# A two-layer attention and top-2 expert kernel: expert sums fetched token by token through device memory, and V projected last in layer 0

## The chip, the cores and the metric

The kernel runs on one core of one Trainium2 chip. The metric is the device time of the whole program in microseconds (us): lower is better. A measurement of this kernel can tell some 2% from no change.

## The reference

256 tokens (a 16x16 grid) of 192 numbers go through two layers. Each layer is attention with 12 heads of 16, then a mixture of 8 experts, of which each token uses its best two:

```python
x = x + conv0(ln(x))        # qkv, scores + relative position terms (rows, columns), softmax, projection
t = ln(x); x = x + t + sum_e w_e * down_e(silu(gate_e t) * up_e t)      # layer 0: hidden 432 ... 1584
x = x + conv1(ln(x))        # the same attention without relative terms
t = ln(x); x = x + t + sum_e w_e * (w2_e relu(w1_e t + b1_e) + b2_e)    # layer 1: hidden 768 each
```

Here w_e is the router's softmax value of a chosen expert (in layer 1 divided by the sum of the two), and 0 for the six others. All data are float32.

## The kernel before, in words

Everything is written by hand for five engines, each with its own instruction list, and the only ties are semaphores. TensorE (PE) does all products. An f32 matmul shows as two records in the trace, a transpose as one.

**Attention.** `attend` projects K, Q and V with `project` and `project_tokens`. In layer 0, 32 small products (L1036) then form the relative position terms from Q, one for each row and each column of the grid, 48 columns each, in banks 5, 6, 7 and 3. ScalarE (ACT) copies the row terms (L503), VectorE (DVE) adds the column terms (L655) and rounds (L657), GpSimd (POOL) makes the remainder (L424), and only then may `scores` (L970) start. `keep_clock` (L916) puts products of ones into places where PE would idle. Then, two heads at a time: scores, row maximum on DVE (L661), exponential on ACT (L517), transposes (L985), copies, and `weigh` (L997), the product with V.

**Experts.** The router's two choices per token give each token a place in its expert's list of at most 96 `SLOTS`. `gather` (L1122) collects the tokens of each expert by products with one-hot matrices. Then the experts run in steps of 128 hidden units (layer 0: 60 steps; layer 1: 8 x 3 steps of 256), written as (e, t). A step on PE is `first_products` (L1135, L1137, L1139) and, `LAG` steps later, `down` (L1150). ACT and DVE make the hidden values in between (L475, L750 in layer 0; L481, L753 in layer 1). When an expert's sum is complete, DVE copies it out of PSUM (L739, `copy_y`), and PE brings it back to the tokens in `combine` (L1158): two products with `weightedT`, the one-hot matrix times the router's weight, into bank 4, where the sum over experts is kept. POOL makes those matrices for all 8 experts (L435), PE transposes them two experts at a time (L1167, `turn_weighted`), and DVE and ACT copy them (L732, L464).

An expert with over 96 tokens gets a further job in layer 1; in these data there is one (three more steps at the end). Which jobs there are is found on DVE beside the first steps: `list_jobs`, `number_jobs` (L787 to L795), `place_jobs`. SyncE (SP) issues all DMAs in the order of its list; in layer 1 it reads the job list and loads the job's weights.

## Time and profile before

| | us |
|---|---|
| median of 3 runs | 238.82 (236.95 to 240.77) |
| the profiled execution | 235.63 |
| its span, first to last instruction | 233.6 |
| PE busy | 216.7 (93%) |
| DVE busy | 103.6 (44%) |
| ACT busy | 68.5 (29%) |
| POOL busy | 37.0 (16%) |
| mean granted TensorE clock | 0.957 of full speed |

The profile is of one execution; its time includes 2.0 us outside the span. Busy time of matmuls is modelled and overlaps, so differences between the starts of instructions say more than their durations.

### The profile page before, as it was taken

The page shows a single profiled execution, that of the slowest core. Times are in us where ns is not written, and L with a number is a line of the kernel's source. Part 1 is how long each engine was busy: PE and PEld are TensorE (multiplying, and loading weights), DVE is VectorE, ACT ScalarE, POOL GpSimd, SP SyncE. Part 2 cuts the span into 40 slices and gives each one's busy share as a digit, 9 for nine tenths or more (in the row PEclk, how much of TensorE's full clock was granted, in tenths as well). Part 3 has the DMA queues.
Part 4 walks back from the last instruction along what each step waited for, and adds up shares of the span by engine and source line. Part 5 has one row for each costly group of instructions (what it writes and reads, how often), then busy time and mean ns, then how long its engine had stood idle before and what let it go on. Part 6 is the DMA issues. An engine that isn't in the chain of part 4 may idle for free.

```text
span 233.6 us, 4218 instructions
## 1 busy us (share of the span) xinstructions
PE 216.7 (93%) x1580; PEld 195.1 (84%) x1580; DVE 103.6 (44%) x334; ACT 68.5 (29%) x197; POOL 37.0 (16%) x60
## 2 busy tenths in 40 slices
PE   7999989869999999999999989799869999999992
PEld 7799877549898999999999789575558999999991
DVE  2340687568623122222222234886569564723221
ACT  2031087525221212222222131666522021211100
POOL 5220300011990000000000014000014950000000
PEclk9996799997999999999999999958999999999997
DMA  6999999936000000000000000999900000500001
GB/s 169 349 425 423 438 454 424 440 140 153 0 3 0 3 0 0 3 1 0 3 0 0 3 6 15 369 425 426 385 6 1 0 0 15 191 0 3 0 3 41
DMA packets 4492, 31.05 MB, mean 133 GB/s; under 512 B 584, under 2 KB 2064, under 8 KB 2192
## 3 DMA queue, kind: packets, MB, share of 16 engines
q1 hardware_dynamic: 4464, 30.69, 33.6%
q8 instruction: 15, 0.25, 0.5%
q14 instruction: 13, 0.11, 0.1%
HBM read 30.50 MB, written 0.20 MB: 131 GB/s over the span
## 4 chain that ended last, share of the span: by engine, by line
PE 90%; ACT 4%; issue 2%; DVE 2%; POOL 0%; DVEq 0%; ACTq 0%; POOLq 0%
PE bank L1150 17%; PE bank L1137 13%; PE bank L916 9%; PE bank L1135 8%; PE bank L1139 7%; PE bank L985 6%; PE bank L1158 5%; PE bank L940 5%; PE bank L1036 4%; PE bank L970 4%; PE bank L997 3%; PE bank L1122 3%; PE bank L1167 1%; ACT scratch L517 1%; DVE neg_max L661 1%
## 5 line engine op out<-in xcount | busy, mean ns | idle before, releaser
L1150 PE MATMUL bank<-w,scratch 128*96 128x192 f32 (+2 forms) x228 | 52.0, 330 | 0.1
L1137 PE MATMUL bank<-xe_lo,w 128*128 128x192 f32 (+3 forms) x168 | 43.3, 339 | 0.0
L750 DVE TENSOR_TENSOR scratch<-scratch,bank 128x96 f32<-128x96 f32 (+5 forms) x60 | 15.2, 253 | 52.8 <-ACT scratch L475 52.8
L1150 PEld LDWEIGHTS bank<-w,scratch 128*96 128x96 f32 (+2 forms) x228 | 30.7, 164 | 1.5 <-issue 0.3
L475 ACT ACTIVATE scratch<-bank 128x96 f32<-128x96 f32 (+5 forms) x60 | 15.0, 249 | 55.3 <-PE bank L1139 55.3
L1135 PE MATMUL bank<-scratch,w 128*128 128x96 f32 (+3 forms) x168 | 30.8, 265 | 0.0
L1135 PEld LDWEIGHTS bank<-scratch,w 128*128 128x128 f32 (+3 forms) x168 | 27.7, 185 | 3.0 <-issue 3.0
L1139 PE MATMUL bank<-scratch,w 128*128 128x96 f32 (+3 forms) x168 | 29.9, 259 | 0.0
L1139 PEld LDWEIGHTS bank<-scratch,w 128*128 128x128 f32 (+3 forms) x168 | 29.0, 185 | 0.4
L517 ACT ACTIVATE scratch<-bank,neg_max 128x256 f32<-128x256 f32 x48 | 19.8, 477 | 18.9 <-DVE neg_max L661 18.9
L1137 PEld LDWEIGHTS bank<-xe_lo,w 128*128 128x128 f32 (+3 forms) x168 | 24.9, 187 | 0.0
L435 POOL TENSOR_SCALAR scratch<-const,place,gate 128x96 f32<-128x96 f32 x32 | 22.0, 702 | 5.2 <-issue 5.1
L916 PE MATMUL bank<-ones 128*128 128x128 f32 x134 | 21.4, 327 | 1.4 <-POOL ones L393 1.4
L404 POOL TENSOR_TENSOR rstd<-var_eps,const 128x2 f32<-128x2 f32 x4 | 2.8, 706 | 119.8 <-DVE var_eps L593 119.8
L916 PEld LDWEIGHTS bank<-ones 128*128 128x128 f32 x134 | 20.3, 239 | 1.4 <-POOL ones L393 1.4
L985 PE MATMUL bank<-const,scratch 128*128 128x128 f32 x96 | 16.4, 307 | 3.8 <-ACT scratch L517 1.7
L661 DVE TENSOR_REDUCE neg_max<-bank 128x2 f32<-128x512 f32 x24 | 15.7, 683 | 6.5 <-PE bank L970 6.5
L985 PEld LDWEIGHTS bank<-const,scratch 128*128 128x128 f32 x96 | 11.3, 152 | 8.3 <-ACT scratch L517 4.2
L481 ACT ACTIVATE scratch<-bank,bias 128x96 f32<-128x96 f32 x24 | 6.9, 336 | 32.2 <-PE bank L1139 32.2
L753 DVE TENSOR_SCALAR scratch<-bank,bias 128x96 f32<-128x96 f32 x24 | 6.5, 313 | 17.6 <-PE bank L1139 17.5
L1158 PE MATMUL bank<-scratch 96*128 96x192 f32 x64 | 13.1, 327 | 0.4 <-DVE scratch L739 0.4
L671 DVE COPY scratch<-bank 128x512 f32<-128x512 f32 x16 | 10.9, 684 | 3.5 <-PE bank L985 3.5
(160 smaller groups left out, 254.4 us busy)
## 6 DMA issues: line engine op xcount, KB each, us to landing
w<-experts_dram SPq DMA_DIRECT2D x9, 1152.0 KB, 12.3
w<-experts_dram SPq DMA_DIRECT2D x1, 3624.0 KB, 41.8
w<-experts_dram SPq DMA_DIRECT2D x1, 3024.0 KB, 33.7
w<-experts_dram SPq DMA_DIRECT2D x1, 2496.0 KB, 26.6
w<-experts_dram SPq DMA_DIRECT2D x1, 2016.0 KB, 21.2
w<-experts_dram SPq DMA_DIRECT2D x1, 1704.0 KB, 16.9
w<-experts_dram SPq DMA_DIRECT2D x1, 1416.0 KB, 12.2
w<-experts_dram SPq DMA_DIRECT2D x1, 1272.0 KB, 9.3
```

What stands on the lines that cost most here:

```text
L435: nc.gpsimd.tensor_scalar(weighted[:, t, e, :], places, place[:, t, e:e + 1], gate[:, t, e:e + 1], ALU.is_equal, ALU.mult).then_inc(weight ...
L475: nc.scalar.activation(silu_g[0:m, n % 2, :], up_bank(n)[0:m, 0], ACT.Silu).then_inc(sems["silu_ready"], 1)
L517: nc.scalar.activation(probs[:, h % HB, t, :], bank[h % HB][:, t * TOK:(t + 1) * TOK], ACT.Exp, bias=neg_max[:, h, t:t + 1]).then_inc(prob ...
L661: nc.vector.tensor_reduce(neg_max[:, h, :], bank[h % HB][:].rearrange("p (t k) -> p t k", t=TT), AX_X, ALU.max, negate=True).then_inc(max_ ...
L750: nc.vector.tensor_tensor(hidden[0:m, n % RING, 0], silu_g[0:m, n % 2, :], up_bank(n)[0:m, 1], ALU.mult).then_inc(sems["hidden_vec"], 1)
L916: nc.tensor.matmul(bank[b][:, 0:P], ones[:], ones[:], start=True, stop=True)
L985: last = nc.tensor.transpose(bank[4 + head % 2][:, at:at + P], probs[:, h % HB, t, k * P:(k + 1) * P], ident)
L1135: nc.tensor.matmul(tile[:, 0], w0[:, begin + long[0]:begin + long[0] + m], hi, start=True, stop=False, skip_group_check=True)
L1137: nc.tensor.matmul(tile.rearrange("p u s -> p (u s)"), w0[:, begin + short:begin + short + m], lo.rearrange("p u s -> p (u s)"), start=Fal ...
L1139: return nc.tensor.matmul(tile[:, 1], w0[:, begin + long[1]:begin + long[1] + m], hi, start=False, stop=True, skip_group_check=True)
L1150: ins = nc.tensor.matmul(y_bank(e)[0:SLOTS, 0:C], hidden[0:m, n % RING, u], w0[0:m, begin + at:begin + at + C], start=t == 0 and u == 0, s ...
L1158: ins = nc.tensor.matmul(bank[4][:, t * C:(t + 1) * C], turned[0:SLOTS, t * P:(t + 1) * P], y_out[0:SLOTS, e % 2, :], start=first and t == ...
```

## The change: sums of six experts through device memory, V last in layer 0

For the experts 0 to 5 (`DIRECT = 6`) of both layers, `combine` is gone. DVE copies each expert's sum to a row block of its own (`y_out` has 8), and SP stores it to a table in device memory (`memory_rows`, 96 rows for each expert and a row of zeros). DVE computes, for both choices of each token, the number of its row (`find_rows`, at step (2, 0)) and its weight (`gate_picks`, at (3, 0)). When all six blocks are stored, POOL fetches with four indirect DMAs, one for each half of the tokens and each choice, 128 rows of 768 bytes each. DVE multiplies and adds them to the tokens (`add_fetched`): in layer 0 one at each of the steps (7, 5) to (7, 8), in layer 1 all four behind the last hidden values of the first job (or at the end, without a job). Experts 6 and 7, and the job, are combined as before.

In layer 0, Q is now projected before K, the relative products follow, and V comes last. The relative products read 96 columns each (two grid lines, of which the second is overwritten by the next product), except the last one of each axis. DVE adds column terms half by half. `keep_clock` before the scores does 2 products instead of 10 in layer 0. In both layers 4 products of ones stand behind the scores of the first four heads, V's bias is added on DVE behind the third row maximum, and PE waits for V only at its first use.

```diff
+DIRECT = 6
+ZERO_ROW = DIRECT * SLOTS
...
-KEEP_START, KEEP_SCORES, KEEP_ROUTE, KEEP_PLACE, KEEP_NORM = 12, (10, 7), 6, 5, 16
+KEEP_START, KEEP_SCORES, KEEP_FIRST, KEEP_ROUTE, KEEP_PLACE, KEEP_NORM = 12, (2, 7), 4, 6, 5, 16
...
+        TURN_AT = (1, 0)
+        ROWS_AT, GATES_AT = (2, 0), (3, 0)
+        ADD_AT = (E - 1, 5)
...
+            return y_out[0:SLOTS, e if main and e < E else DIRECT + e % 2]
...
+            sp.dma_start(att[0:CH, :, W_Q:W_K], weights[0][:, :, W_Q:W_K]).then_inc(q_landed, 16)
             sp.dma_start(att[0:CH, :, W_K:W_V], weights[0][:, :, W_K:W_V]).then_inc(k_landed, 16)
-            sp.dma_start(att[0:CH, :, W_Q:W_K], weights[0][:, :, W_Q:W_K]).then_inc(q_landed, 16)
+            sp.dma_start(rel_t[:], rel_in).then_inc(rel_landed, 16)
...
+            def store_rows(layer, some):
+                for e in some:
+                    sp.wait_ge(main[layer]["y_ready"], e + 1)
+                    sp.dma_start(memory_rows[layer][e * SLOTS:(e + 1) * SLOTS, :], y_out[0:SLOTS, e]).then_inc(rows_landed[layer], 16)
...
+            store_rows(0, range(DIRECT))
...
+            store_rows(1, range(2))
+            jobs(sp, load_job, lambda k: store_rows(1, range(2, DIRECT)) if k <= JOB_ROOMS else None)
...
-                    for e in range(E):
+                    for e in range(DIRECT, E):
...
+                    pool.wait_ge(rows_ready, layer + 1)
+                    pool.wait_ge(rows_landed[layer], 16 * (DIRECT + 1))
+                    for i in range(TT * 2):
+                        nc.gpsimd.indirect_dma_start(fetched[:, i], None, memory_rows[layer],
+                                                     bass.IndirectOffsetOnAxis(ap=row_index[:, i:i + 1], axis=0)).then_inc(fetched_landed[layer], 16)
...
+                def add_v():
+                    dve.wait_ge(v_psum, layer + 1)
+                    dve.wait_ge(par_landed, 16)
+                    for t in range(TT):
+                        nc.vector.tensor_tensor(v1[:, t, :, 0:HD], bank[6][:, t * C:(t + 1) * C].rearrange("p (h d) -> p h d", d=HD),
+                                                par[:, layer, B_V:B_V + C].rearrange("p (h d) -> p h d", d=HD), ALU.add).then_inc(v_ready, 1)
...
+                    for half, b in enumerate((7, 3)):
+                        dve.wait_ge(rel_psum, 3 + half)
+                        for g in range(HG):
...
+                            if half == 1:
+                                dve.wait_ge(rel_ready, HG + g + 1)
+                                nc.vector.tensor_copy(rel_hi[:, g], relT[:, g]).then_inc(rel_rounded, 1)
...
+                    if h == 2:
+                        add_v()
...
+            def find_rows(layer):
+                step(nc.vector.tensor_scalar(fits[:], place[:, :, 0:DIRECT], float(SLOTS), None, ALU.is_le))
+                step(nc.vector.scalar_tensor_tensor(row_of[:], small[:, 4:4 + DIRECT].unsqueeze(1).to_broadcast([P, TT, DIRECT]), float(SLOTS),
+                                                    place[:, :, 0:DIRECT], ALU.mult, ALU.add))
+                step(nc.vector.scalar_tensor_tensor(row_of[:], row_of[:], -1.0 - ZERO_ROW, fits[:], ALU.add, ALU.mult))
+                step(nc.vector.tensor_tensor(by_pick[:, :, :, 0:DIRECT], hits[:, :, :, 0:DIRECT],
+                                             row_of[:].unsqueeze(2).to_broadcast([P, TT, 2, DIRECT]), ALU.mult))
+                step(nc.vector.tensor_reduce(row_sum[:], by_pick[:, :, :, 0:DIRECT], AX_X, ALU.add))
+                nc.vector.tensor_scalar(row_index[:].rearrange("p (t j) -> p t j", t=TT), row_sum[:], float(ZERO_ROW), None,
+                                        ALU.add).then_inc(rows_ready, 1)
+            def gate_picks():
+                step(nc.vector.tensor_tensor(by_pick[:], hits[:], gate[:].unsqueeze(2).to_broadcast([P, TT, 2, E]), ALU.mult))
+                step(nc.vector.tensor_reduce(pick_gate[:].rearrange("p (t j) -> p t j", t=TT), by_pick[:], AX_X, ALU.add))
+            def add_fetched(layer, i):
+                into = (acc, x[:])[layer][:, i // 2, :]
+                if i == 0:
+                    dve.wait_ge(fetched_landed[layer], 16 * TT * 2)
+                    if layer == 0:
+                        dve.wait_ge(acc_ready, 1)
+                step(nc.vector.scalar_tensor_tensor(into, fetched[:, i], pick_gate[:, i:i + 1], into, ALU.mult, ALU.add))
...
+                    if end == "main" and (e, t) == ROWS_AT:
+                        find_rows(layer)
+                    if end == "main" and (e, t) == GATES_AT:
+                        gate_picks()
+                    if end == "main" and layer == 0 and e == ADD_AT[0] and 0 <= t - ADD_AT[1] < 2 * TT:
+                        add_fetched(0, t - ADD_AT[1])
+                    if end == "first job" and t == STEPS1 - 1:
+                        for i in range(2 * TT):
+                            add_fetched(1, i)
...
+                if g == 0:
+                    pe.wait_ge(v_ready, TT * (layer + 1))
...
+                    project_q()
+                    pe.wait_ge(k_landed, 16)
+                    project_k()
...
-                            last = nc.tensor.matmul(bank[banks[i // 8]][:, at:at + HG * GRID], window, lines[:, i],
+                            wide = 1 if i + 1 == GRID else 2
+                            last = nc.tensor.matmul(bank[banks[i // 8]][:, at:at + wide * HG * GRID], window, lines[:, i:i + wide],
...
-                pe.wait_ge(v_ready, TT * (layer + 1))
+                keep_clock(KEEP_FIRST, 5)
...
-                    if t == lag + 1 and e >= 1:
-                        combine(layer, sems, e - 1, weightedT[:, e - 1], layer == 0 and e == 1, False)
...
+                    if t == lag + 1 and e > DIRECT:
+                        combine(layer, sems, e - 1, weightedT[:, e - 1 - DIRECT], layer == 0 and e - 1 == DIRECT, False)
+                    if (e, t) == TURN_AT:
+                        turn_weighted(layer)
```

What that does to the lists of instructions is shown for the three places that matter. First PE at the start of layer 0, from the projections to the first scores; before:

```order
L940 MATMUL bank0<-xnT,att 128x256 x4
L940 MATMUL bank1<-xnT,att 128x256 x2
L940 MATMUL bank2<-xnT,att 128x256 x4
L940 MATMUL bank3<-xnT,att 128x256 x2
L946 MATMUL bank4<-att,xnT 128x192 x4
L1036 MATMUL bank5<-scratch,rel_t 128x48 x8
L1036 MATMUL bank6<-scratch,rel_t 128x48 x8
L1036 MATMUL bank7<-scratch,rel_t 128x48 x8
L1036 MATMUL bank3<-scratch,rel_t 128x48 x8
L916 MATMUL bank1<-ones 128x128 x10
```

and in the changed kernel:

```order
L1016 MATMUL bank2<-xnT,att 128x256 x4
L1016 MATMUL bank3<-xnT,att 128x256 x2
L1016 MATMUL bank0<-xnT,att 128x256 x4
L1016 MATMUL bank1<-xnT,att 128x256 x2
L1113 MATMUL bank5<-scratch,rel_t 128x96 x8
L1113 MATMUL bank6<-scratch,rel_t 128x96 x7
L1113 MATMUL bank6<-scratch,rel_t 128x48
L1113 MATMUL bank7<-scratch,rel_t 128x96 x8
L1113 MATMUL bank3<-scratch,rel_t 128x96 x7
L1113 MATMUL bank3<-scratch,rel_t 128x48
L1022 MATMUL bank6<-att,xnT 128x192 x4
L992 MATMUL bank1<-ones 128x128 x2
```

V (L946, now L1022) has moved behind the relative products, and eight products of ones are gone.

Second, DVE in layer 1 from the hidden values of step (2, 0) to those of (2, 2); before:

```order
L753 TENSOR_SCALAR scratch<-bank,bias 128x96 x2
L732 COPY scratch<-bank 96x512
L739 COPY scratch<-bank 96x192
L787 TENSOR_SCALAR w<-w 128x5
L788 SCALAR_TENSOR_TENSOR w<-w 128x5
L789 TENSOR_SCALAR w<-w 128x5
L790 TENSOR_TENSOR w<-const,w 128x40
```

and in the changed kernel (L812 is the hidden values, L798 the copy of an expert's sum):

```order
L812 TENSOR_SCALAR scratch<-bank,bias 128x96 x2
L770 TENSOR_SCALAR fits<-place 128x12
L771 SCALAR_TENSOR_TENSOR row_of<-const,place 128x12
L773 SCALAR_TENSOR_TENSOR row_of<-row_of,fits 128x12
L774 TENSOR_TENSOR by_pick<-hits,row_of 128x4x6
L776 TENSOR_REDUCE row_sum<-by_pick 128x4
L777 TENSOR_SCALAR row_index<-row_sum 128x4
L798 COPY scratch<-bank 96x192
L857 TENSOR_SCALAR w<-w 128x5
L858 SCALAR_TENSOR_TENSOR w<-w 128x5
```

Six dependent operations stand where one copy stood. Third, POOL from the norm ahead of layer 0's experts to the norm of layer 1; before:

```order
L404 TENSOR_TENSOR rstd<-var_eps,const 128x2
L435 TENSOR_SCALAR scratch<-const,place,gate 128x96 x16
L441 TENSOR_TENSOR o_tok<-x,xn 128x384
L404 TENSOR_TENSOR rstd<-var_eps,const 128x2
L407 TENSOR_TENSOR rstd<-var_eps,const 128x2
```

and in the changed kernel:

```order
L434 TENSOR_TENSOR rstd<-var_eps,const 128x2
L465 TENSOR_SCALAR scratch<-const,place,gate 128x96 x4
L471 TENSOR_TENSOR o_tok<-x,xn 128x384
L475 DMA scratch<-memory_rows,row_index 128x192 x4
L434 TENSOR_TENSOR rstd<-var_eps,const 128x2
L437 TENSOR_TENSOR rstd<-var_eps,const 128x2
```

Twelve matrices are gone and four indirect fetches have come, ahead of the next layer's norm.

## Rows read from the trace of the kernel before

**Rows 1.** The chain that ended last, by engine, shares of the span.

```profile
PE 90%; ACT 4%; issue 2%; DVE 2%; POOL 0%; DVEq 0%; ACTq 0%; POOLq 0%
```

**Rows 2.** Stretches: length, busy us (instructions) of each engine, granted clock, DMA, GB/s.

```profile
14.18:19.05 4.87, 4.87 (x44) 4.87 (x44) 1.81 (x5) 2.00 (x5) 0.00 (x0) 1.00 1.04 437
19.05:23.60 4.55, 4.55 (x24) 4.55 (x23) 0.00 (x0) 0.00 (x0) 0.00 (x0) 0.50 1.01 427
151.36:165.44 14.08, 13.42 (x105) 9.06 (x105) 9.90 (x17) 9.50 (x24) 0.00 (x0) 0.76 1.01 425
31.15:43.77 12.62, 12.38 (x137) 9.16 (x137) 9.76 (x17) 9.40 (x24) 0.00 (x0) 1.00 1.02 438
59.94:131.90 71.96, 71.96 (x519) 68.11 (x518) 19.20 (x70) 15.88 (x61) 9.60 (x14) 1.00 0.00 1
180.87:228.20 47.33, 47.23 (x332) 46.31 (x332) 20.22 (x77) 8.59 (x28) 9.14 (x14) 1.00 0.08 26
```

**Rows 3.** The same chain in order of time, layer 1's experts: start, length, what.

```profile
187.51 0.44 PE bank L1167 x4
...
190.74 0.65 PE bank L1158 x4
```

**Rows 4.** Instructions in order of time, start of layer 0: start, us, engine, line.

```profile
12.57 1.46 PE L946 MATMUL bank<-att,xnT 96*128 96x192 f32 x8
14.18 9.41 PE L1036 MATMUL bank<-scratch,rel_t 128*128 128x48 f32 x64 [0.15 <-ACT scratch L496]
23.40 3.65 PE L916 MATMUL bank<-ones 128*128 128x128 f32 x20
24.64 0.77 DVE L655 SCALAR_TENSOR_TENSOR scratch<-bank,const,scratch 128x128 f32<-128x128 f32 x2
25.45 0.30 DVE L657 CAST parts<-scratch 128x256 fp32r<-128x256 f32 x1
25.89 0.74 POOL L424 TENSOR_TENSOR parts<-scratch,parts 128x256 fp32r<-128x256 f32 x1 [0.29 <-DVE parts L657]
26.98 0.50 PE L970 MATMUL bank<-parts 32*128 32x256 f32 x4
```

**Rows 5.** The same view, layer 1, PE around its first scores.

```profile
147.66 0.76 PE L970 MATMUL bank<-parts 32*128 32x256 f32 x16
150.09 1.34 PE L985 MATMUL bank<-const,scratch 128*128 128x128 f32 x8 [1.67 <-issue]
```

**Rows 6.** The same view, layer 1, DVE at steps (2, 0) to (2, 2).

```profile
192.23 0.54 DVE L753 TENSOR_SCALAR scratch<-bank,bias 128x96 f32<-128x96 f32 x2
...
193.87 0.34 DVE L739 COPY scratch<-bank 96x192 f32<-96x192 f32 x1
194.13 0.16 DVE L787 TENSOR_SCALAR w<-w 128x5 f32<-128x5 f32 x1
...
195.56 0.16 DVE L795 CAST job_regs<-w 1x6 int32<-1x6 f32 x1
195.65 0.54 DVE L753 TENSOR_SCALAR scratch<-bank,bias 128x96 f32<-128x96 f32 x2
```

**Rows 7.** The same view, PE: down product of step (2, 2), layer 1.

```profile
197.25 0.82 PE L1150 MATMUL bank<-w,scratch 128*96 128x192 f32 x4
```

**Rows 8.** The same view, DVE: expert 5's copy and the later deadline, both layers.

```profile
108.10 0.35 DVE L739 COPY scratch<-bank 96x192 f32<-96x192 f32 x1
...
124.77 0.25 DVE L750 TENSOR_TENSOR scratch<-scratch,bank 128x96 f32<-128x96 f32 x1 [0.82 <-ACT scratch L475]
...
215.14 0.34 DVE L739 COPY scratch<-bank 96x192 f32<-96x192 f32 x1
...
226.23 0.54 DVE L753 TENSOR_SCALAR scratch<-bank,w 128x96 f32<-128x96 f32 x2 [1.79 <-PE bank L1139]
228.19 0.35 DVE L739 COPY scratch<-bank 96x192 f32<-96x192 f32 x1 [1.41 <-PE bank L1150]
```

**Rows 9.** DMA issues: KB each, us from issue to landing.

```profile
out_dram<-x SPq DMA_DIRECT2D x1, 192.0 KB, 2.8
```

**Rows 10.** In order of time: the nearest two-operand adds and POOL's largest operation.

```profile
169.31 0.74 DVE L688 TENSOR_TENSOR x<-x,par 128x192 f32<-128x192 f32 x2
...
68.55 0.99 POOL L441 TENSOR_TENSOR o_tok<-x,xn 128x384 f32<-128x384 f32 x1
```

More of the change, by code:

```diff
@@ L224, in metaformer_kernel @@
         moe_done = sem("moe_done")
+        rows_landed = [sem(f"rows_landed{layer}") for layer in range(2)]
+        fetched_landed = [sem(f"fetched_landed{layer}") for layer in range(2)]
+        rows_ready = sem("rows_ready")
         redo_step, stats_redone, rstd_redone, xn_redone = (sem(s) for s in ("redo_step", "stats_redone", "rstd_redone", "xn_redone"))
@@ L772, in stream @@
                 dve.wait_ge(sems["hidden_used"], ns[-1] + 1)
-                copy_y(sems, e)
+                if layer == 1 and e >= E:
+                    dve.wait_ge(sems["combined"], e - 1 - DIRECT)
+                    nc.vector.tensor_copy(y_room(e, True), y_bank(e)[0:SLOTS, 0:C]).then_inc(sems["y_ready"], 1)
+                else:
+                    copy_y(sems, e, end == "main")
             def list_jobs():
@@ L891, in job, with finish_jobs @@
                             copy_job(k)
-                        stream(1, main[1], steps_of(1, E + k), "job")
-                    jobs(dve, job, lambda k: dve.wait_ge(main[1]["combined"], E + k))
+                        stream(1, main[1], steps_of(1, E + k), "job" if k else "first job")
+                    def finish_jobs(k):
+                        if k == 0:
+                            for i in range(2 * TT):
+                                add_fetched(1, i)
+                        dve.wait_ge(main[1]["combined"], LATE + k)
+                    jobs(dve, job, finish_jobs)
             dve.wait_ge(x_landed, 16)
```

135 lines of the change are left out of this document (61 added, 74 removed).

## The prediction

> **What bounds the kernel now.** I read the chain of waits first. PE makes 90% of it [rows 1], so work taken from PE shortens the kernel wherever nothing else is late. The table of stretches then says where that holds: over layer 0's experts PE is busy for all 71.96 us and over layer 1's for 47.23 of 47.33 us, while DVE works 19.20 and 20.22 us [rows 2]. The same table shows where PE runs at half its clock: 4.55 us of the relative products at a granted 0.50, and layer 1's attention at a mean of 0.76 against 1.00 in layer 0's [rows 2]. These are the two levels, 1.2 and 2.4 GHz.
>
> **Removed from the experts.** A combine inside the stream costs PE 0.65 us and the transposes of one pair of experts 0.44 us [rows 3]; both are steps of the chain itself, not durations that overlap. Six combines and three pairs go in each layer: 12 x 0.65 + 6 x 0.44 = 10.4 us. The copies and POOL's matrices that go too (12 of 16 per layer) were hidden. Nothing that is left waits for them.
>
> **Added on DVE in layer 1.** The hidden values of step (2, 2) must be there when PE comes to their down product, which started at 197.25 [rows 7]. By then two pairs of transposes (0.88) and two combines (1.30) will be gone, so PE wants them at 195.07. DVE's chain from step (2, 0) now is: hidden values 0.50, six operations of `find_rows`, the copy of expert 1's sum 0.26, the eight operations of `number_jobs`, hidden values 0.54. The eight took 194.13 to 195.65, 0.19 us each [rows 6], so the six take 1.15. The chain started at 192.23 [rows 6] behind `list_jobs`, which comes 0.44 earlier with the first transposes gone: 191.79 + 0.50 + 1.15 + 0.26 + 1.52 + 0.54 = 195.76, and a tenth until PE sees it. PE waits about **0.8 us**. Bounds: 0 if the small operations go faster on 12 numbers, 1.5 if each takes 0.3. In layer 0 DVE uses 19.20 of 71.96 us and two steps lie between a hidden value and its use; 1.15 us is hidden there. `gate_picks`, two operations, has a step without hidden values to itself in layer 1. SP's list has the stores of experts 0 and 1 ahead of the job's weights; both sums are copied by 194.2, before the job list is there at 195.65 [rows 6], so the job's load isn't late.
>
> **The fetch and its deadline.** The path is: expert 5's sum copied, SP stores it, POOL waits for that and issues four fetches, DVE waits for all four. Queued behind this wait on DVE are only the adds and later hidden values in layer 0, and the last copy in layer 1, for which PE's last combine waits. In layer 0 the copy ended at 108.45 and the hidden values of (7, 5) at 125.02 [rows 8]; with one combine between them gone the deadline is 15.9 us. In layer 1 it is 215.48 to 226.77, less 0.65: 10.6 us [rows 8]. No indirect DMA and no store of this size is in the trace. The nearest DMA is the output store, 2.8 us from issue to landing for 192 KB [rows 9]; a fetch is 98 KB. POOL's part of a fetch isn't shown either; its longest operation takes 0.99 us [rows 10]. If all four overlap: 2.8 + 2.8 = 5.6 us. If each waits for the one before: 2.8 + 4 x 2.8 = 14.0. I take POOL as held 0.9 us by each issue and the landings as overlapping, since POOL's list has no wait between them: 2.8 + 3 x 0.9 + 2.8 = 8.3 us. That is in time in both layers; upper bound 3.4 us late in layer 1 alone.
>
> The Trainium skill, "DMA: Bandwidth & Descriptors", section "Anatomy of one DMA — SWDGE (gpsimd) path", has a fixed cost of about 2.0 us for each such DMA plus its bytes at 436 GB/s, mostly waiting for the write to be confirmed. By it, as an estimate, a fetch of 98 KB takes 2.2 us, and four in a row behind a 2.8 us store 11.7 us, 1.1 us late in layer 1. No run here shows it yet.
>
> The four adds stand behind the hidden values that ended at 226.77. Two adds in place took 0.74 [rows 10], so four take 1.5, up to 228.3, where the last copy started at 228.19 [rows 8]: **+0.1 us**. In layer 0 one add a step is hidden.
>
> **The start of layer 0.** Before: V 12.57, relative products 14.18 to 23.40, products of ones, scores at 26.98 [rows 4]. 40 of the 64 records lie in the 4.87 us at full clock, 0.12 us each, and 24 in the 4.55 us at half, 0.19 us each [rows 2]. After: the relative products follow the projections directly, at 12.57 (Q is now first, and its copies on ACT run beside K's products). A product of twice the columns in 0.12 us costs nothing if the weights bound it; the same weights with 128 columns, the products of ones at half clock, take 0.18 us a record [rows 4], no more than the 48 columns did. So 64 x 0.12 = 7.7 us, to 20.25, if the clock holds. It fell after 4.9 us of products that each streamed 48 columns, and with 96 PE streams twice the share of the time; dense stretches like the experts' hold 1.00 throughout [rows 2]. V took 1.46 [rows 4], ones four records of at most 0.18: scores at 22.3. The other condition is column term 0.39, rounding 0.30, remainder on POOL 0.74 [rows 4]: 20.25 + 1.4 + waits = 21.9. It is hidden by V. Gain 26.98 - 22.3 = **4.7 us**. If V had stayed in front, the cover would be gone and the 1.4 exposed. Bounds: 6.0 if a record takes 0.1; 2.4 if the clock falls as before, see below. Moving the load of Q ahead of K and of the relative table ahead of V's delays none of them: the first projection's weights are still the first to be loaded, and the table is first used at 12.57.
>
> **Layer 1's first heads.** Between the first scores (147.66 + 0.76) and the first transposes (150.09) PE had 1.67 us without work [rows 5], and its clock is at half for a part of what follows. Now four products of ones fill that, 8 records of 0.12, done before 150.09 and so free. If the clock holds, the stretch 151.36 to 165.44 (14.08 us) becomes like layer 0's 12.62 us, which has more score products but the same 9.8 to 9.9 us of DVE [rows 2]. I take 12.1, **2.0 us** gained; bounds 0 and 3.3. V's bias, two operations of 0.3 us, moves into a DVE gap of about 0.45 us in both layers: +0.15 each, **+0.3**.
>
> **Sum.** 10.4 + 4.7 + 2.0 - 0.8 - 0.1 - 0.3 = 15.9 us off the profiled 235.63: 219.7. The three runs lie 1.3 to 5.1 us above the profiled execution. I read that as more time at half clock in them; the change takes away two such places, so I add back 0.8 rather than 3.2: **220.5 us**.
>
> **Rivals.**
> Fetches one behind another, or held up on POOL by DVE: 14.0 us against a deadline of 10.6. Against it: DVE does little in that stretch, two copies and three pairs of hidden values, all read from PSUM. For it: nothing in the trace shows that POOL issues quickly. 3.4 late: 223.9 us. 20%.
> The Trainium skill, "SBUF — State Buffer", section "A bandwidth-pool intuition that's wrong (but worth ruling out)", has a gpsimd DMA of 620 ns that took 3100 ns beside a DVE copy, since its descriptors could not be written. By it, as an estimate, four take 12.4 us and are 4.6 late, 225.1 us; the copies that it speaks of go from SBUF to SBUF, and none here does.
>
> The clock falls all the same: at 19.05, 54 of the 64 relative records are done; ten more at 0.19 and V at twice 1.46 bring the scores to 24.6, 2.3 later, and layer 1 gains nothing, 2.0: 224.8 us. 20%. For it: the granted clock follows what PE did before, and layer 1's rows show it fall in a stretch with PE busy 13.42 of 14.08 us.
>
> Everything better: clock at 1.00 throughout, and the 0.8 kept: 216 us. 6%.
>
> Slower than before: row-wise fetching. One mechanism, POOL making its 512 rows one by one. Both deadlines are then missed, layer 0's from T = 15.9 and layer 1's from 10.6. To lose the 18.3 us gained against the median, (T - 15.9) + (T - 10.6) = 18.3, T = 22.4 us, or 38 ns a row after the 2.8 us store; for 2% more than before, T = 24.8, 43 ns a row: 243.6 us. POOL's longest operation, 384 numbers in each of 128 partitions, takes 0.99 us [rows 10], which speaks against 4.9 us for the 128 row numbers of a fetch. 4%.
>
> **How the numbers follow.** Forecast 50%, the rivals as above. The range must leave out at most 2 in 10; 215.5 to 227 holds the forecast, its bounds, both likely rivals and half of their sum. A change of 2% is about what this kernel's measurement can tell: 4.8 us. All cases but row-wise fetching are faster by more than that: faster 0.95, same 0.01, slower 0.04.
>
> **What the profile of the changed kernel would show.** Relative products in about 7.7 us at a granted 1.00, scores at 22.3; the expert stretches shorter by 5.2 and 4.4 us with PE still busy throughout; a PE gap below 1 us at step (2, 2) of layer 1; the fourth fetch landing 8.3 us after expert 5's copy; no DVE wait for fetches in either layer. Wrong would make it: a DVE gap in front of the adds, with PE's last combine behind it; the clock at 0.50 in the relative products or the first heads; or relative products that take longer with 96 columns at full clock.

## The result and the profile after

| | us |
|---|---|
| before, median of 4 runs beside it | 239.45 (236.95 to 240.77) |
| after, median of 4 runs | 224.78 (222.77 to 227.16) |
| ratio | 0.939, 95% interval 0.926 to 0.952 |
| profiled execution, before and after | 235.63, 222.77 |

Ratios and means in this document count only executions within 1.5% of the fastest of the same kernel (of those above, 227.16 and 240.77 don't count, their granted clock being lower), and the profiled executions of three experiments (sums alone, 48 columns, no ones behind the first scores) don't count either, so that their clock isn't used as evidence.

The same chain as [rows 1], of the changed kernel:

```profile
PE 56%; DVE 10%; issue 4%; DMA 3%; ACT 2%; POOL 1%; POOLq 1%; DVEq 0%
```

PE had 90% of it. The chain now leaves PE for a long way, over the fetch and DVE, which says only that it passes there; how late PE really is stands in the stages. First the stretches that answer to [rows 2], with the same columns and between the same instructions: the relative products; layer 0's experts (71.96 us before); layer 1's heads behind the first (14.08 before); its route up to `gather`; its experts up to the start of the last copy (47.33 before).

```profile
12.95:21.62 8.67, 8.67 (x65) 8.67 (x64) 5.21 (x12) 1.16 (x2) 2.35 (x3) 1.00 1.01 426
55.61:122.38 66.77, 66.77 (x483) 62.97 (x483) 20.27 (x80) 15.36 (x60) 5.74 (x7) 1.00 0.05 14
141.83:153.91 12.08, 10.73 (x105) 7.22 (x105) 9.70 (x17) 9.30 (x24) 0.00 (x0) 1.00 1.02 429
156.19:167.02 10.83, 8.72 (x57) 7.54 (x56) 7.39 (x36) 3.10 (x10) 0.69 (x1) 0.84 0.29 121
170.09:213.56 43.47, 42.37 (x298) 41.26 (x296) 21.65 (x87) 8.03 (x27) 4.94 (x6) 1.00 0.17 48
```

The granted clock (the first number behind the engines) is 1.00 where it was 0.50 and 0.76 before. It is 0.84 in a place where nothing was changed, the route of layer 1. The same stretch of the kernel before:

```profile
167.71:177.13 9.42, 7.32 (x57) 6.06 (x56) 6.60 (x33) 3.09 (x10) 0.69 (x1) 1.00 0.13 52
```

The last row above holds what went wrong: PE is busy 42.37 of 43.47 us, where it had hardly a gap before (47.23 of 47.33).

The start of layer 0 in order of time, as in [rows 4]:

```profile
12.95 8.85 PE L1113 MATMUL bank<-scratch,rel_t 128*128 128x96 f32 x64
21.62 1.53 PE L1022 MATMUL bank<-att,xnT 96*128 96x192 f32 x8
22.98 0.61 PE L992 MATMUL bank<-ones 128*128 128x128 f32 x4
23.61 0.50 PE L1046 MATMUL bank<-parts 32*128 32x256 f32 x4
```

The relative products take 8.67 us at a full clock, not the 7.7 of the prediction, and the scores start at 23.61 instead of 26.98. Layer 1, PE around its first scores, as in [rows 5]:

```profile
138.12 0.76 PE L1046 MATMUL bank<-parts 32*128 32x256 f32 x16
138.81 1.16 PE L992 MATMUL bank<-ones 128*128 128x128 f32 x8
140.51 1.39 PE L1061 MATMUL bank<-const,scratch 128*128 128x128 f32 x8 [0.54 <-ACT scratch L551]
```

The ones fill most of the gap: 0.54 us of 1.67 are left. DVE and PE at step (2, 2), as in [rows 6] and [rows 7]:

```profile
181.39 0.16 DVE L770 TENSOR_SCALAR fits<-place 128x12 f32<-128x12 f32 x1
...
182.43 0.17 DVE L777 TENSOR_SCALAR row_index<-row_sum 128x4 uint32<-128x4 f32 x1
...
184.29 0.54 DVE L812 TENSOR_SCALAR scratch<-bank,bias 128x96 f32<-128x96 f32 x2
...
183.06 0.82 PE L1236 MATMUL bank<-w,scratch 128*96 128x192 f32 x4
184.88 0.89 PE L1236 MATMUL bank<-w,scratch 128*96 128x192 f32 x4 [0.26 <-DVE scratch L812]
```

`find_rows` takes 1.2 us as foreseen. The down products are 1.82 us apart, where steps without this wait are 1.40 apart: PE lost 0.4 us.

The chain in order of time from expert 5's copy in layer 1 to the last combine. It is the fetch, term by term:

```profile
200.53 0.28 DVE scratch L798
200.80 0.02 issue
200.82 3.39 DMA memory_rows<-scratch
204.21 0.02 issue
204.24 0.02 POOLq L473
204.25 0.72 issue
204.97 1.10 POOL scratch L475
...
207.63 0.95 POOL scratch L475
208.57 0.30 issue
208.88 2.84 DMA scratch<-memory_rows,row_index
211.72 0.02 issue
211.74 0.43 DVE x L792
...
213.56 0.37 DVE scratch L841
213.92 1.52 issue
215.44 0.59 PE bank L1244 x2
```

And the same place in order of time on DVE and PE, which answers to the last lines of [rows 8]. First the last combine of the kernel before, whose copy ran from 228.19 to 228.54:

```profile
228.60 0.92 PE L1158 MATMUL bank<-scratch,w 96*128 96x192 f32 x4 [0.45 <-DVE scratch L739]
```

The changed kernel:

```profile
211.74 1.78 DVE L792 SCALAR_TENSOR_TENSOR x<-scratch,pick_gate,x 128x192 f32<-128x192 f32 x4 [0.31 <-DMA scratch<-memory_rows,row_index]
211.99 0.81 PE L1236 MATMUL bank<-w,scratch 128*96 128x192 f32 x4
213.56 0.35 DVE L841 COPY scratch<-bank 96x192 f32<-96x192 f32 x1
215.44 0.92 PE L1244 MATMUL bank<-scratch,w 96*128 96x192 f32 x4 [2.64 <-issue]
217.25 0.42 SPq L416 DMA_DIRECT2D out_dram<-x  x1
```

Three things are to be seen. From the copy to the fourth landing it is 10.9 us, and DVE waits 0.31 us for it. The four adds then take 1.78 us and hold up the copy of the job's sum. And PE's last combine doesn't follow that copy, as it did before by 0.06 us, but 1.5 us later, with "issue" as its releaser: PE waited for nothing that a semaphore shows.

The account, by the starts of the same instructions in the two profiled executions (before, after, how far the difference grew in that stage):

| | before | after | stage |
|---|---|---|---|
| first scores, layer 0 | 26.98 | 23.61 | -3.4 |
| first expert product, layer 0 | 59.94 | 55.61 | -1.0 |
| last combine, layer 0 | 133.74 | 124.21 | -5.2 |
| first expert product, layer 1 | 180.87 | 170.09 | -1.3 |
| last down product | 227.34 | 211.99 | -4.6 |
| last combine, layer 1 | 228.60 | 215.44 | +2.2 |
| store of the output | 230.41 | 217.25 | 0.0 |

With 0.3 us more outside these marks that is the 12.9 us between 235.63 and 222.77.

### The profile page after: what moved, and what is told of

It reads as the page before. It is cut to its first block, busy times and chain, and to the rows that moved or that the text cites. A ratio compares the mean times of both kernels' runs of the same rounds, so it can differ in the third digit from the quotient of the medians.

```text
span 220.5 us, 4078 instructions
## 1 busy us (share of the span) xinstructions
PE 202.6 (92%) x1508; PEld 182.1 (83%) x1508; DVE 107.2 (49%) x354; ACT 67.4 (31%) x195; POOL 29.2 (13%) x44
## 4 chain that ended last, share of the span: by engine, by line
PE 56%; DVE 10%; issue 4%; DMA 3%; ACT 2%; POOL 1%; POOLq 1%; DVEq 0%
PE bank L1236 13%; PE bank L1223 12%; PE bank L1221 7%; PE bank L1225 6%; PE bank L992 4%; PE bank L1016 2%; PE bank L1061 2%; PE bank L1208 2%; DMA memory_rows<-scratch 2%; PE bank L1075 1%; DMA scratch<-memory_rows,row_index 1%; DVE neg_max L697 1%; PE bank L1244 1%; POOL scratch L475 1%; DVE scratch L812 1%
## 5 line engine op out<-in xcount | busy, mean ns | idle before, releaser
L992 PEld LDWEIGHTS bank<-ones 128*128 128x128 f32 x134 | 19.8, 231 | 1.6 <-POOL ones L423 1.4
L475 POOL DMA_INDIRECT scratch<-memory_rows,row_index x8 | 8.0, 999 | 80.4 <-DMA memory_rows<-scratch 78.6
L1061 PE MATMUL bank<-const,scratch 128*128 128x128 f32 x96 | 15.1, 284 | 2.3 <-ACT scratch L551 1.3
L1061 PEld LDWEIGHTS bank<-const,scratch 128*128 128x128 f32 x96 | 10.1, 140 | 7.0 <-ACT scratch L551 5.7
L812 DVE TENSOR_SCALAR scratch<-bank,bias 128x96 f32<-128x96 f32 x24 | 6.5, 313 | 15.2 <-PE bank L1225 15.1
L1016 PE MATMUL bank<-xnT,att 96*128 96x256 f32 x48 | 10.8, 382 | 1.3 <-ACT xnT L483 1.3
L709 DVE COPY scratch<-bank 128x512 f32<-128x512 f32 x16 | 10.9, 682 | 2.3 <-PE bank L1061 2.3
```

What stands on the lines that cost most here:

```text
L709: nc.vector.tensor_copy(probsT[:, head % TRING], bank[4 + head % 2][:]).then_inc(probsT_vec, 1)
L992: nc.tensor.matmul(bank[b][:, 0:P], ones[:], ones[:], start=True, stop=True)
L1016: last = nc.tensor.matmul(out_ap, att[0:CH, half, at:at + P], xnT[0:CH, half, :], start=half == 0, stop=half == 1)
L1061: last = nc.tensor.transpose(bank[4 + head % 2][:, at:at + P], probs[:, h % HB, t, k * P:(k + 1) * P], ident)
```

## Experiments

Each was timed against the kernel before, on the same chip. Ratios are to that. They were timed in four sets, of which only the kernels of one set stood side by side: the first four below; near code, 64 waits, split adds with near code and rows later; split adds with far code, ones in the route and columns; all together. The kernel before took 234.0 to 243.7 us in them, so differences of one or two per cent between sets are within the noise. Where profiles are compared, the tail means the time from the last down product to the last combine and from there to the output store: 1.26 + 1.81 us before, 3.45 + 1.81 after.

### The two parts alone

One kernel has only the attention's part of the diff (attention alone), the other (sums alone) only the expert sums' part (`DIRECT`, `store_rows`, `find_rows`, `gate_picks`, the fetches and adds).

> Only the changed attention (Q first, relative products 96 wide, V last, ones behind the first scores, V's bias late); the expert sums are combined by one-hot products as before. Theory 'the two parts add up': the attention's share of the gain is the start of layer 0 (-3.4 us in the profile of the changed kernel) and layer 1's first heads (-2.0), so about 5.4 us under the kernel before, ratio 0.977. Rival 'one part carries the other': since the granted clock follows what PE did before, the attention alone may be worth up to 9 us or nothing. Profile: scores of layer 0 at 23.6, granted clock 1.00 up to there, the tail (last down product to last combine) as before, 1.3 us.

Measured: 232.17 us median (230.8 to 232.87), ratio 0.988, interval 0.978 to 0.999. Profile to profile it is 4.8 us under the kernel before (230.8 against 235.63). Scores at 23.2, tail 1.26 + 1.81.

> Only the sums through device memory; the attention of both layers is as before. Theory 'the two parts add up': 10.4 us of combines and transposes less about 2.4 us in the tail of layer 1, so 8 us under the kernel before, ratio 0.966, scores of layer 0 at 27.0 as before. Rival: all of the difference of the medians (14.7 us) less the attention's share, 9.3 us. If the tail's gap in front of the last combine comes from the fetches, it is here too; if it comes from where the code lies, it may be gone or longer.

Measured: 236.65 median (227.95 to 237.93). Only one of the four executions counts, 227.95, 7.7 us under the mean of the kernel before in this set (235.7). Tail 2.88 + 2.53.

On the same footing, mean to mean, the attention alone gave 3.7 us (232.0 against 235.7), less than the 5.4 of its theory and than the 4.8 from profile to profile. The parts come to 11.4 or 12.5 us, against 12.9 for both in the profiles: they add up as far as this can tell, the second part on one execution only, and neither carries the other. The profiles show the parts more directly. The stretch of layer 0's experts, first product to last combine, is 73.8 us before and with attention alone, and 68.6 with the sums alone and with both. The gap in the tail came with the sums' part.

### What keeps the clock in the attention

```diff
-wide = 1 if i + 1 == GRID else 2
+wide = 1
```

> The changed kernel with relative products of 48 columns as before; V last, all else as changed. Theory 'the width keeps the clock': the granted clock falls to 0.50 in the relative products, they take 9.2 us or more instead of 8.7, and V and the first scores run slow too: 1 to 2.3 us slower than the changed kernel, 226 us. Rival 'V last keeps it, the width only costs': clock 1.00, 64 records of 0.12 us, 7.7 us instead of 8.7, so 1 us faster, 223.8.

Measured: 225.79 median (225.29 to 232.72, 5 runs), ratio 0.958, interval 0.944 to 0.972. The three runs that count took 225.3 to 225.8 against 222.8 to 225.2 of the changed kernel: 1.4 us more on the mean, within what this can tell. The profiled execution shows the fall at the place expected (4.06 us at 1.00, then 5.73 at 0.50), but doesn't count. So this run doesn't settle the width; the kernel before shows only that 48 columns can lose the clock there [rows 2], with V in front of them. That the width keeps the clock is not shown. Tail 3.08 + 2.28.

```diff
-KEEP_START, KEEP_SCORES, KEEP_FIRST, ... = 12, (2, 7), 4, ...
+KEEP_START, KEEP_SCORES, KEEP_FIRST, ... = 12, (2, 7), 0, ...
```

> The changed kernel without the four products of ones behind the scores of the first four heads, in both layers. Theory: they keep layer 1's clock; without them it falls to 0.50 in the first heads of layer 1 and the attention there is 2.0 us longer, 226.8. Rival: the clock holds there without them (its fall in the kernel before came from V in front of the scores, or from chance), no change.

Measured: 228.83 median (225.79 to 230.36), ratio 0.965, interval 0.947 to 0.984; the interval overlaps that of the changed kernel (0.926 to 0.952) a little. Its two runs that count are 2.9 us over those of the changed kernel on the mean, the direction and about the size of the theory; the ones stand in both layers, and which layer lost how much can't be read from a profile that doesn't count. What can be read is that in all eleven kernels with these ones the stretch of layer 1 from its first projection to its second output product took 28.96 to 28.98 us, and 30.96 in the kernel before. Unexpected: the tail is 1.57 + 1.81, so the 2.9 us may be more than that without this help.

```profile
223.88 0.92 PE L1244 MATMUL bank<-scratch,w 96*128 96x192 f32 x4 [0.76 <-DVE scratch L841]
```

Here PE's last combine does follow the copy, by 0.06 us, though only eight products of ones, far ahead of it, were left out.

### What PE waits for at the end

The branch behind the job's last down product leads, if there is no second job, over the code of four further jobs to the last combine. In the first experiment that combine follows directly; it is called near code here, the other order far code. The edit, on PE alone, without the flag that chooses between the two orders:

```diff
-                with eng.If(number > k):
-                    body(k)
-                    rest(k + 1)
-                with eng.Else():
-                    otherwise(k)
+                with eng.If(number < k + 1):
+                    otherwise(k)
+                with eng.Else():
+                    body(k)
+                    rest(k + 1)
```

> The changed kernel with the branches of the jobs turned round on PE alone: where there is no further job, PE's last combine is the code that follows directly, instead of lying behind the code of four more jobs. Nothing else is changed. Theory 'PE waits for its code': the 2.6 us in front of the last combine, in which no semaphore is waited for, are the fetch of far code; the combine now follows the copy of the last sum by 0.1 us, 1.5 us faster. Rival 'every taken jump costs': the jump is now at the job's start and costs 2 to 3 us there, no gain or slower. Rival 'not the code': the gap stays, no change.

Measured: 220.51 median (220.0 to 225.16), ratio 0.938, interval 0.932 to 0.944.

The second puts 64 fulfilled waits at the start of PE's list:

```diff
             keep_clock(KEEP_START)
+            for _ in range(64):
+                pe.wait_ge(ones_set, 3)
```

> The changed kernel with 64 waits that are already fulfilled at the start of PE's list, where PE is idle: the code of all that follows lies 64 instructions later. Theory 'what counts is where a 16 KB block of code ends': the block whose fetch starts at 212.40 in the changed kernel is fetched at another time, and the gap in front of the last combine changes by over 0.5 us. Rival 'the jump itself starts the fetch': the gap stays 2.6 us, from last down product to last combine 3.4 us.

Measured: 223.52 median (222.66 to 224.59), ratio 0.952, interval 0.944 to 0.959. These two stood side by side: the means are 220.3 and 223.6, and the two intervals just don't meet (0.9435 and 0.9444). Tail 3.23 + 2.54: the shift by 64 instructions didn't help. Against the changed kernel, in another set, the ratios tell nothing (0.938 and 0.939); what the near code is worth there is read from the profiles. The kernel with near code, in order of time:

```profile
212.26 1.78 DVE L799 SCALAR_TENSOR_TENSOR x<-scratch,pick_gate,x 128x192 f32<-128x192 f32 x4 [0.69 <-DMA scratch<-memory_rows,row_index]
214.07 0.35 DVE L848 COPY scratch<-bank 96x192 f32<-96x192 f32 x1
214.48 0.92 PE L1251 MATMUL bank<-scratch,w 96*128 96x192 f32 x4 [1.54 <-DVE scratch L848]
216.29 0.42 SPq L423 DMA_DIRECT2D out_dram<-x  x1
```

The releaser is DVE again, 0.06 us behind the end of the copy. Profile to profile it is 2.3 us under the kernel with the 64 waits: 1.6 us are the tail, 0.7 a first projection that started earlier (7.28 against 8.03). Against the changed kernel the tail is 1.1 us shorter, not the 1.5 of the theory, since DVE waited 0.69 us for the fetch here, against 0.31. The rival of a jump that costs at the job's start is out: from layer 1's first expert product to the last down product it takes 41.97 us, against 41.90.

The last experiment of this kind moves two of the four adds behind the copy and leaves the branch as it was:

```diff
                     if end == "first job" and t == STEPS1 - 1:
-                        for i in range(2 * TT):
+                        for i in range(2):
                             add_fetched(1, i)
...
                     nc.vector.tensor_copy(y_room(e, True), ...)
+                    if end == "first job":
+                        for i in range(2, 2 * TT):
+                            add_fetched(1, i)
```

> The changed kernel with two of layer 1's four adds moved behind the copy of the job's sum, and the branches as in the changed kernel. It parts the two costs in the tail. Theory 'PE's code comes late, whatever DVE does': the copy ends at 1.5 us behind the start of the last down product, the combine starts 2.9 to 3.4 us behind it all the same, and then the two last adds are hidden, so last down product to output store stays 5 us or more; 223.5 us. Rival 'the adds in front of the copy set the combine': it follows the copy by 0.1 us, as in the kernel with split adds and near code, 3.7 us from last down product to store.

Measured: 223.56 median (222.27 to 224.54), ratio 0.940, interval 0.925 to 0.955: no gain over the changed kernel. (Near code with the same split, below, has the same ratio in another set, 220.93 us; the times alone don't part the two.) The chain of its tail, and under it the granted clock of the last down product and of the last combine (columns as in the stretches):

```profile
214.17 0.67 PE bank L1239 x4
214.84 0.04 DVEq L840
214.87 0.04 issue
214.92 0.36 DVE scratch L841
215.28 1.82 issue
217.10 1.66 PE bank L1247 x4
```

```profile
214.01:214.82 0.81, 0.81 (x5) 0.49 (x4) 0.62 (x2) 0.00 (x0) 0.00 (x0) 1.00 0.08 20
217.10:218.76 1.66, 1.65 (x4) 1.14 (x4) 0.00 (x0) 0.00 (x0) 0.00 (x0) 0.50 0.14 25
```

The copy is ready 1.27 us behind the start of the last down product, the combine starts 3.1 behind it all the same. That decides it: DVE doesn't set this wait. The second fence adds a cost: PE was idle, and the combine ran at half its clock, 1.66 us for 0.92. With the 64 waits and here, both with far code, it was so (2.5 us from combine to store); in none of the six kernels with near code.

Far code alone doesn't make the gap, though. The kernel before, the attention alone and the kernel without ones behind the first scores have the same branch over four jobs, and in them the combine follows the copy by 0.05 to 0.06 us. It is late in the five others with far code: from last down product to last combine 3.45 us (changed kernel), 2.88 (sums alone), 3.08 (48 columns), 3.23 (64 waits) and 3.09 (here), and in none of the six with near code, 1.31 to 2.36.

The DMA view shows a packet of 16 KB of an instruction queue at 212.40 in the changed kernel, 0.4 us behind the start of its last down product, and at the same distance in the four others that are late; here is its window of 212 to 213, and the near-code kernel with split adds in 211.8 to 213.4, the same place:

```profile
q8 instruction: 1, 0.02, 8.7%
```

```profile
DMA packets 0, 0.00 MB, mean 0 GB/s; under 512 B 0, under 2 KB 0, under 8 KB 0
```

In the six kernels with near code none comes between the last down product and the start of the last combine. In the kernels of before and with attention alone, which have no gap, the packet came 1.7 and 1.4 us before the last down product. That fits code which is fetched too late, 2.4 to 3.0 us ahead of its use, but what the packet holds isn't shown. What it doesn't explain is the kernel without ones behind the first scores: its packet comes 0.6 us behind the last down product, and its combine isn't late, 1.0 us behind the packet.

### The tail with near code, and the rows later

Near code with the same split of the adds:

> As the kernel with the branches turned round, and in layer 1 two of the four adds stand before the copy of the job's sum and two behind it, beside the last combine. Theory 'two costs in the tail, one behind the other: four adds in front of the copy, then the code': the copy starts at about 212.85 instead of 213.56, the combine at 213.3 instead of 215.44, in all 2.1 us under the changed kernel. If the code's fetch isn't removed by turning the branches round, no gain at all from moving the adds.

Measured: 220.93 median (220.21 to 224.3), ratio 0.940, interval 0.934 to 0.945. Tail 1.57 + 2.17 = 3.74 against 2.36 + 1.81 = 4.17 of the near code alone: 0.4 us better in the profile, nothing in the times. The last addition starts 1.53 us behind the combine instead of 1.16. The two adds behind the copy end before that; what holds DVE for the 0.4 us is not shown, its own branches perhaps.

```diff
-        ROWS_AT, GATES_AT = (2, 0), (3, 0)
+        ROWS_AT, GATES_AT = ((2, 0), (5, 0)), (3, 0)
```

> As the kernel with split adds, and in layer 1 the six operations that find the row numbers come at step (5, 0) instead of (2, 0). Theory: PE's wait at step (2, 2) goes, 0.3 to 0.5 us, and nothing waits at (5, 0), where DVE has a free step. Rival: DVE's other work (lists of jobs) sets that wait anyway, no change. Limit of the measurement: a difference of 0.4 us is read from the profile, not from the times.

Measured: 221.24 median (219.9 to 221.82), ratio 0.941, interval 0.933 to 0.949: no difference in time, as announced. From the first expert product to the last down product of layer 1 it takes 41.47 us, against 41.97 with the rows at (2, 0) and 41.90 in the changed kernel: the wait of 0.5 us was `find_rows`.

### The clock in the route, and the column axis

In each of the eight counted profiled executions with the changed attention and without what follows here, the clock was below 1.00 in the route of one layer or the other, or of both: from the router's product to `gather` it took 3.7 us at full clock and 5.1 to 6.7 otherwise. The kernel before lost it there too, in layer 0 (5.13 us, in the changed kernel 3.71), and not in layer 1 (3.72, in the changed kernel 5.12). The changed kernel's row 156.19:167.02 above is one. Two idle stretches stand ahead of it, where PE waits for x and for the transposed x:

```diff
+KEEP_ADDED, KEEP_TURNED = 2, 3
...
+                if n % 2 == 1:
+                    keep_clock(KEEP_ADDED)
...
+                if n % 2 == 1:
+                    keep_clock(KEEP_TURNED)
```

The first stands in front of the transposes of x, the second behind them; all else is as with the rows later.

> As the kernel with the row numbers at (5, 0), with two products of ones in front of the transposes of the sum x and three behind them, in both layers, where PE waits for DVE and ACT between the attention and the router. Theory 'those idle stretches let the clock fall in the products of ones of the route': it holds at 1.00 there, and the 1.5 to 3 us that the route is longer in the layer where it fell are gone: 219.3 us, mean granted clock over 0.990 in most runs. Rival: the fall is pushed to another place, no change of the time.

Measured: 218.62 median (218.45 to 219.47), ratio 0.922, interval 0.909 to 0.935, with a mean granted clock of 0.995 to 1.000 in all four executions, where the kernel without it had 0.971 to 0.992. Both routes in this kernel (layer 0's, layer 1's) are at full clock:

```profile
43.68:51.56 7.88, 7.13 (x57) 6.29 (x57) 5.84 (x29) 2.95 (x9) 0.69 (x1) 1.00 0.93 356
155.70:165.10 9.40, 8.41 (x67) 7.34 (x66) 6.59 (x33) 3.08 (x10) 0.69 (x1) 1.00 0.33 136
```

9.40 us stand against 10.83 with the clock at 0.84: 1.4 us, about the lower end of the theory. In the kernel that this one was built from, the rows later, it was layer 0's route that lost the clock: 6.08 us from the router's product to `gather`, and 3.70 here, which is about the difference of the two profiled executions (220.76 and 218.45).

The other kernel built from the rows later has no such ones, but column terms of 48 columns:

```diff
-wide = 1 if i + 1 == GRID else 2
+wide = 1 if axis == 1 or i + 1 == GRID else 2
```

> As the kernel with the row numbers at (5, 0), and the relative products of the column axis 48 wide again (those of the row axis 96). Theory 'reading 96 columns across the grid's columns costs, 0.15 us a record against 0.12': if the clock holds, the 64 records take 7.7 us instead of 8.7, V starts 1 us earlier, 220 us. Rival 'the width holds the clock': with the second half narrow, it falls to 0.50 in it or in V, and the start loses 1 to 2 us, 222.5. Third: no gain at full clock either, since the reading of the column axis costs 0.15 at either width.

Measured: 221.85 median (217.77 to 223.53), ratio 0.936, interval 0.922 to 0.951. Its relative products in the profiled execution, which is the one at 217.77 and the only one that counts:

```profile
12.51:19.60 7.09, 7.09 (x65) 7.08 (x64) 5.20 (x12) 1.16 (x2) 2.36 (x3) 1.00 1.02 426
```

7.09 us for 64 records, 1.6 less than with 96 columns on both axes. So 96 columns read across the grid's columns cost more than 48, by 0.05 us a record. The changed kernel shows the two rates side by side: 11 records in each us from 14 to 16, in the row axis, and 8 in each from 17 to 21, in the column axis. It is the first theory, with 0.6 us more than it expected. The three others had a mean clock of 0.960 to 0.969.

> The kernel with the ones in the route, and the relative products of the column axis 48 wide. Theory 'the ones in the route hold the clock whatever comes before': 1.5 us taken from 218.6, 217.0 us, mean granted clock over 0.99 in most runs. Rival 'the narrow second half lets the clock fall in most runs': as in the kernel before this one with that change alone, of which three of four runs had a mean clock of 0.960 to 0.969, so 221 us in most runs, and one or two at 217; then 96 columns are the better choice for both axes.

Measured over six executions: 218.48 median (216.96 to 221.92), ratio 0.920, interval 0.914 to 0.926. Four took 216.96 to 219.1, two 221.4 and 221.9 with a mean clock of 0.972. The median equals that of 96 columns (218.62): the lowest is 1.5 us lower, but the clock is less sure. Neither theory wins outright. These two are the fastest versions of the study, 6 us under the changed kernel by the medians and 4 to 5 by the ratios (0.922 and 0.920 against 0.939); the first one's interval overlaps that of the changed kernel, the second one's just doesn't.

## Why the prediction was right

The forecast of 220.5 us lies 4.3 under the median; 224.78 is inside the range of 215.5 to 227, and faster by over 2% it is. The time alone doesn't speak for the forecast: it lies nearer to two rivals (224.8 with the clock falling in the old places, 223.9 with fetches one behind another), and neither of their mechanisms came. By its own steps, against the profiled execution (219.7 foreseen, 222.77 measured):

**Combines and transposes, 10.4 us.** Held. Layer 0's experts are 5.20 us shorter, of 5.22 foreseen; layer 1's 4.6, with DVE's lateness at step (2, 2) taken off. That term was mis-sized: 0.8 foreseen, 0.4 to 0.5 measured.

**Start of layer 0, 4.7 us.** 3.4 measured. The clock held; the wrong term is "64 x 0.12 = 7.7 us". The argument was that 48 more columns hide behind the weights. For the row axis they do, for the column axis they don't: 7.09 against 8.67 us with that axis at 48 and at 96. The rate was misread too: the row with 4.87 us has 44 records [rows 2], not 40, so 0.11 us each, and 64 of them are 7.1 us. The slip hid 0.6 of the 1.6 us that the column axis cost. The prediction named this as something that would make it wrong. The other 0.4 us is a first projection that started that much later, 7.70 against 7.31. The rest of layer 0's attention and route gave 1.0 us that wasn't foreseen: in layer 0's route the clock fell before (5.13 us) and not in this execution (3.71). That is luck.

**Layer 1's first heads, 2.0 us, and V's bias, 0.3.** The stretch foreseen at 12.1 us took 12.08, and the attention from the projections on is 2.0 us shorter (28.97 against 30.96), but the clock then fell in the route, which cost 1.4 (9.42 before, 10.83 after). The stage gave 1.3 us. The fall in layer 1 and the one that is gone in layer 0 about cancel. That the fall moves to another place was in no rival: "the clock falls all the same" priced the old places only.

**The fetch, 8.3 us against a deadline of 10.6.** 10.9 measured, 0.31 us late: the forecast "in time in both layers" is wrong in layer 1, by little. The rival with 14.0 is wrong in its mechanism: POOL's four issues start 1.25 to 1.41 us apart, and a fetch lands 2.6 to 3.4 us after its issue (median of the eight 2.8; the last one 2.84), so they overlap, as forecast. The missing 2.6 us are in small terms: the store 3.39 for 2.8, POOL's start 0.75 behind the store for nothing, and 3.91 from the first to the fourth issue for 2.7. The Trainium skill, "DMA: Bandwidth & Descriptors", section "Anatomy of one DMA — SWDGE (gpsimd) path", was drawn on for an estimate of 11.7 us: near in its sum, since the estimate's terms erred in both directions, 2.2 us for one fetch against 2.84 here, and four one behind the other where the trace has them overlap. The Trainium skill's "SBUF — State Buffer", section "A bandwidth-pool intuition that's wrong (but worth ruling out)", would have such a DMA take several times longer beside DVE's copies; POOL took 0.94 to 1.21 us for every one of the eight, so no run here shows it.

**The last copy, +0.1 us.** The step that failed most. Measured from last down product to last combine: +2.2 us. The four adds took 1.78 instead of 1.5 and started 0.31 late, which makes 0.7 us up to the end of the copy. The larger part, 1.5 us, is a wait that the prediction had in no form: PE's code for the last combine. With that code near, the combine follows the copy; with the copy early and the code far, it doesn't. That the order of the code decides is shown by turning the branch round; that PE waits there for code to be fetched is argued from the packets, not shown. Why three kernels with the same far code had no gap is open, one of them only eight products of ones away from the changed kernel, and so is what the instruction queue's packet holds.

**The median.** 0.8 us were added for the clock. The median of the four runs is 2.0 above the profiled execution, with a mean clock of 0.957 to 0.987: more of it was spent at half clock than in the profiled one; where, these three runs don't show. With five more products of ones in each layer the mean clock was 0.995 or more in all four executions, but with 48 columns on the column axis beside them it was 0.972 in two of six.

## What to carry to other kernels

A path over device memory is a sum of small terms (store, wake-up, four issues, landing), each here longer than its nearest relative in the old trace; set its deadline with a third to spare, and don't put its last additions in front of the one copy that the end waits for. If the likely way out of a branch leads over much code, write that way first, directly behind the test. When a change removes idle time at one place and the clock holds there, look at the next idle place too: here five products of ones filled two, and the route kept its clock in both layers.

## What the runs showed of the hardware

- A float32 product of 96 columns, read as two grid rows (contiguous), took no longer than one of 48 (0.11 us a record); read as two grid columns it made 32 records 1.6 us longer (8.67 against 7.09 us at a granted clock of 1.00).
- An indirect fetch of 128 rows of 768 bytes took POOL 0.94 to 1.21 us to issue, 0.30 us passed to the next issue, and the last of layer 1's four landed 2.84 us behind its start. The store of 96 such rows took 3.39 us in layer 1, where the four fetches came behind it.
- The order of an engine's code can hold it: PE's first instruction behind a branch over four unused jobs started 2.9 to 3.45 us behind the start of its last product in five kernels, up to 1.8 us after what it needed was there. In three with the same branch, and in all six with the branch turned round, it followed its data by 0.05 to 0.06 us.
- Behind 2.3 and 2.4 us without work, PE's last combine ran at a granted 0.50 in two kernels (1.65 us); behind 2.6 us in the changed kernel it ran at full clock (0.92).
